# Experts' rows turned by a transposing transfer instead of TensorE and a copy

## The reference

```python
xn = _layernorm(x)
# attention: 16 heads of width 32, latent width 128, causal softmax, two output maps
attn = _L0_attn_ref(xn, Wq, Wdkv, Wuk, Wuv, ln_g, ln_b, Wo_h, Wo, bo)
# experts: 8 experts of 512 x 512, each token takes the mean of its best two
gate_logits = einsum('nsd,de->nse', xn, gate_w) + gate_b
_, top_idx = top_k(gate_logits, 2)
all_out = relu(einsum('nsd,edo->nseo', xn, expert_w) + expert_b)
sel = take_along_axis(all_out, top_idx[..., None], axis=2)
return x + attn + sel.mean(axis=2)
```

## Time and profile before

| | us |
|---|---|
| median of 3 runs | 1585.38 (1584.78 to 1585.88) |
| the profiled execution | 1584.98 |
| its span, first to last instruction | 1583.2 |
| experts' stage, first product to last | 1269.45 to 1494.38 |
| TensorE busy over the span | 1505.3 (95%) |
| VectorE | 1138.1 (72%) |
| ScalarE | 901.9 (57%) |
| GpSimd | 579.8 (37%) |

### The profile page before, as it was taken

How to read it: one execution, slowest core, us unless ns; L and a number is a source line. 1 busy time by engine, 2 the same in 40 slices (tenths; PEclk the granted TensorE clock), 3 DMA queues, 4 the chain that set the end, 5 groups by cost and what they waited for, 6 DMA issues and landing times.

```text
span 1583.2 us, 42974 instructions
## 1 busy us (share of the span) xinstructions
PE 1505.3 (95%) x12544; PEld 809.7 (51%) x12545; DVE 1138.1 (72%) x2385; ACT 901.9 (57%) x1629; POOL 579.8 (37%) x725
## 2 busy tenths in 40 slices
PE   5799989999999999999999999999999999999998
PEld 2788844444444444444444444444444445555443
DVE  4788768887777777777777877777777434444478
ACT  1677736666666666666666666666666733333200
POOL 2444402222454544433222322223222466666400
PEclk8799969999999999999999999999999999999999
DMA  6489861222332223222232223222332256655499
GB/s 157 163 267 269 236 172 56 70 71 62 87 83 71 65 68 93 72 70 65 79 90 67 69 68 95 72 68 64 85 85 72 53 172 216 203 163 171 148 410 358
DMA packets 156337, 198.06 MB, mean 125 GB/s; under 512 B 45280, under 2 KB 94560, under 8 KB 155904
## 3 DMA queue, kind: packets, MB, share of 16 engines
q1 hardware_dynamic: 114720, 98.23, 21.9%
q10 hardware_dynamic: 27936, 61.38, 12.5%
q0 software_dynamic: 13632, 37.87, 7.4%
HBM read 109.13 MB, written 63.12 MB: 109 GB/s over the span
## 4 chain that ended last, share of the span: by engine, by line
PE 78%; DVE 9%; DMA 4%; issue 4%; SPq 3%; ACT 1%; another core or an unknown queue 1%; POOL 1%; DVEq 0%; ACTq 0%; POOLq 0%
PE PS L1342 29%; PE PS L1397 28%; PE PS L1447 11%; PE PS L1471 5%; DVE pm L1131 5%; PE PS L1429 2%; DMA arena<-in_x 1%; SPq L428 1%; DVE mx L1136 1%; SPq L420 1%; DVE mx L1135 0%; DVE arena L993 0%; PE PS L1288 0%; PE PS L1259 0%
## 5 line engine op out<-in xcount | busy, mean ns | idle before, releaser
L1131 DVE TENSOR_REDUCE pm<-PS 128x1 f32<-128x512 f32 (+3 forms) x1280 | 716.5, 601 | 201.6 <-PE PS L1342 190.8
L866 ACT ACTIVATE arena<-PS 128x512 f32<-128x512 f32 (+1 forms) x1152 | 613.5, 574 | 302.1 <-PE PS L1342 278.7
L1342 PE MATMUL PS<-arena 97*64 97x512 f16 (+7 forms) x5120 | 695.2, 353 | 28.6 <-DVE pm L1131 21.0
L1397 PE MATMUL PS<-arena 128*33 128x512 f32 (+3 forms) x2560 | 634.9, 531 | 1.0 <-POOL arena L650 1.0
L1342 PEld LDWEIGHTS PS<-arena 97*64 97x64 f16 (+1 forms) x5120 | 330.4, 110 | 417.3 <-DVE pm L1131 138.4
L650 POOL TENSOR_SCALAR_AFFINE_SELECT arena<-arena 128x256 f32<-128x256 f32 (+1 forms) x256 | 111.1, 434 | 548.9 <-ACT arena L866 547.8
L1397 PEld LDWEIGHTS PS<-arena 128*33 128x33 f32 x2560 | 159.4, 111 | 80.6 <-POOL arena L650 1.7
L1447 PE MATMUL PS<-w_hi,arena 128*128 x576 | 171.5, 379 | 4.1 <-DVE arena L1198 1.8
L885 ACT ACTIVATE arena<-PS 128x1024 f16<-128x1024 f32 x72 | 73.4, 1024 | 148.6 <-remote 109.7
L1342 PE MATMUL PS<-later,deny 128*64 128x128 f16 x1024 | 146.1, 222 | 0.0
L1198 DVE SCALAR_TENSOR_TENSOR arena<-PS,eb_bc 128x512 f32<-128x512 f32 x72 | 49.8, 691 | 119.8 <-remote 61.3
(11 more groups left out here) (174 smaller groups left out, 1283.3 us busy)
## 6 DMA issues: line engine op xcount, KB each, us to landing
comb_hl<-arena SPq DMA_DIRECT2D x256, 64.0 KB
w_hi<-expert_rows ACTq DMA_DIRECT2D x32, 512.0 KB, 7.6
arena<-q_pieces ACTq DMA_DIRECT2D x90, 128.0 KB
arena<-k_pieces ACTq DMA_DIRECT2D x90, 128.0 KB
v_rows<-w_lo SPq DMA_DIRECT2D x8, 1056.0 KB, 7.3
arena<-in_x SPq DMA_DIRECT2D x16, 512.0 KB, 5.8
xn_rows<-arena SPq DMA_DIRECT2D x16, 512.0 KB, 6.2
q_pieces<-w_hi SPq DMA_DIRECT2D x32, 256.0 KB, 5.2
```

The source lines that it names most:

```text
L866: a.activation(probs[kk % 4][:, a_ * CH:a_ * CH + w], PS[:, s2_bank(k, x), 0:w], ACT.Exp, scale=SCALE).then_inc(s["exp_done"], 1)
L1131: v.reduce_max(pm[:, c, r, p:p + 1], PS[:, S1_BANK[n], 0:w], AX).then_inc(s["s1_done"], 1)
L1342: last = t.matmul(PS[h:h + P // 2, bank, cols], lhsT[:, h:h + P // 2], rhs, start=start, stop=stop)
L1397: last = t.matmul(PS[rows_, 6 + c % 2, CH - wds[a]:CH], v_sb[pu % 2][:, j + a, :], probs[pk % 4][:, a * off:a * off + wds[a]], start=p_ in ...
```

## The change

The tile's gathered rows are turned by one DMA transfer, from `x_g[n % 4]` to `xg_T[n % 4]`, issued by ScalarE. TensorE's `turn`, its two pairs of PSUM banks and ScalarE's copy are gone. `xg_T` grows from two buffers to four. ScalarE waits for the gather (`xg_in`) and for the product four tiles before (`z_ps`), then issues. GpSimd's gather waits for the transfer four tiles before (`gT0` to `gT3`, one semaphore for each buffer), TensorE's product for its own. Since two of the four buffers lie where attention has its data, ScalarE waits once, before tile 3, for the last moves of attention (`ot_out`). TensorE's loop takes all 18 passes.

```diff
@@ buffers @@
+        xg_T += [tD(2 * KB * P, f16).rearrange("p (z k c) -> p z k c", z=2, k=KB) for _ in range(AHEAD_G - len(xg_T))]
@@ GpSimd, gather @@
-                pool.wait_ge(s["gt_ps"], count(n - AHEAD_G + 1))
+                if n >= AHEAD_G:
+                    pool.wait_ge(s[f"gT{q}"], count(n // AHEAD_G * 16))
@@ ScalarE @@
-            def turned(n, u):
-                act.wait_ge(s["gt_ps"], count(n + 1))
-                act.wait_ge(s["z_ps"], count(n - 1))
-                a.activation(xg_T[u].rearrange("p z k c -> p (z k c)"),
-                             PS[:, 4 + 2 * u:6 + 2 * u, :].rearrange("p z c -> p (z c)"), ACT.Copy).then_inc(s["gT_done"], 1)
-
-            for n in range(2 * (BESIDE + 1)):
-                turned(n, n % 2)
+            def turned(i, q, ever):
+                act.wait_ge(s[f"xg_in{q}"], (i + 1) * 16)
+                if ever:
+                    act.sem_inc(s["step_at"], 1)
+                act.wait_ge(s["z_ps"], count((i - 1) * AHEAD_G + q + 1))
+                if ever:
+                    act.sem_inc(s["step_at"], 1)
+                act.dma_start_transpose(xg_T[q].rearrange("p z k c -> p (z k) c"), x_g[q]).then_inc(s[f"gT{q}"], 16)
+
+            for n in range(2 * AHEAD_G):
+                if n == AHEAD_G - 1:
+                    for par in range(2):
+                        act.wait_ge(s[f"ot_out{par}"], count(BH * OT_OUT))
+                turned(n // AHEAD_G, n % AHEAD_G, False)
             high_part(BH - 1)
-            with act.Fori(BESIDE + 1, PT // 2) as i:
-                for u in range(2):
-                    turned(i * 2 + u, u)
+            with act.Fori(2, PT // AHEAD_G) as i:
+                for q in range(AHEAD_G):
+                    turned(i, q, True)
@@ TensorE @@
-            def turn(n, i, q):
-
-                u = q % 2
-                pe.wait_ge(s[f"xg_in{q}"], (i + 1) * 16)
-                pe.wait_ge(s["gT_done"], count(n - 1))
-                for z in range(2):
-                    for k in range(KB):
-                        last = t.matmul(PS[:, 4 + 2 * u + z, k * P:(k + 1) * P], x_g[q][:, z * E + k * P:z * E + (k + 1) * P],
-                                        ident16[:], start=True, stop=True)
-                last.then_inc(s["gt_ps"], 1)
-
-            def experts(i, more):
+            def experts(i):
                 for q in range(AHEAD_G):
                     n, u = i * AHEAD_G + q, q % 2
-                    if q < AHEAD_G - 1 or more:
-                        turn(n + 1, i + (q + 1) // AHEAD_G, (q + 1) % AHEAD_G)
                     e = pe.value_load(expert_of[0:1, ds(n, 1)], min_val=0, max_val=NE - 1)
-                    pe.wait_ge(s["gT_done"], count(n + 1))
+                    pe.wait_ge(s[f"gT{q}"], count((i + 1) * 16))
                     pe.wait_ge(s["half_done"], count(n - 1))
...
-                        last = t.matmul(PS[:, u, :], xg_T[u][:, z, k, :],
+                        last = t.matmul(PS[:, u, :], xg_T[q][:, z, k, :],
...
-            turn(0, 0, 0)
             pe.wait_ge(s["ot_done"], count(NC * BH))
-            with pe.Fori(0, PT // AHEAD_G - 1) as i:
-                experts(i, True)
-            experts(PT // AHEAD_G - 1, False)
-
-
-            pe.wait_ge(s["gT_done"], count(PT))
+            with pe.Fori(0, PT // AHEAD_G) as i:
+                experts(i)
```

More of the change, by code:

```diff
@@ L218, in layer_kernel @@
             "cnt_ps routed id_zero id_done ids_in "
-            "xg_in0 xg_in1 xg_in2 xg_in3 gt_ps gT_done z_ps half_done y_done y_st0 y_st1 y_st2 y_st3 "
+            "xg_in0 xg_in1 xg_in2 xg_in3 gT0 gT1 gT2 gT3 z_ps half_done y_done y_st0 y_st1 y_st2 y_st3 "
             "proj_ps acc_done dveE"
```

## The result

The changed kernel takes 1613.45 us (median of 4 runs, 1603.88 to 1618.63) against 1585.63 us for the kernel before beside it: ratio 1.017, 95% interval 1.013 to 1.021. It is 1.7% slower, clear of the noise, and lies above the range of the prediction (1550 to 1602 around 1569). Its profiled execution has a span of 1612.0 us, 28.8 more than before's 1583.2.

What follows compares the result with a forecast made beforehand. TensorE bounds the experts' stage at 3.12 us a tile; without turning, GpSimd's steps (gain 15.9 us) and TensorE's stalled products (gain 14.5) both give about 2.91 a tile, so 1584.98 less 15.5 is 1569, range 1550 to 1602.

Steps and rivals of the forecast that it cites:

- I take 0.80: Experts' stage: a transposing transfer of 256 KB takes 0.80 us of all 16 DMA engines, as a gather does.
- The strided load: Load of ln_g in 4-byte elements, used as upper limit on the transfer's cost: 250 us a tile.
- the sentence from the Trainium skill on equal speed: Transposing transfers run as fast as ordinary ones, 350 to 400 GB/s; the transfer's term would be 0.7 us.
- Landing "3.15": Start of the experts' stage: tile 0's transfer lands 3.15 us after its issue, like a 256 KB load.
- 0.9 us later: Start of the experts' stage: first product at 1270.4 instead of 1269.45, 0.9 us later.
- The stall of 0.64 us in every second tile: TensorE's two product banks: a VectorE signal 2.3 us late stalls TensorE 0.64 us in every second tile.
- 72 x 2.91: TensorE's forecast path through the experts' stage: 72 tiles at 2.91 us, ending at 1479.9 against 1494.38.
- GpSimd's 1.46 us a step: Gathers and scatters in the experts' stage: 133 steps of 1.46 us, 2.92 us a tile.
- the rival of TensorE's bound: Experts' stage: GpSimd's steps stay at 1.28 us and signals come in time; 33 us less, 1552; chance 24%.
- The round trip (14%): Gather plus transfer above 11.6 us makes the ring of four set the pace; at 14 us, 1612; chance 14%.
- The slow blocks' 4 us a tile: Transposing transfer works block by block, not by bytes; at 4 us a tile 1650; chance 12%.
- ScalarE's issues: ScalarE gains 72 transfer issues, taken at 1.23 us each, well below a tile's 2.9.

Runs made afterwards that it cites:

- r4_after: Changed kernel with four product banks in place of two: 1.0234 of the kernel before, 1607.9 us.
- r4_copy: Changed kernel with a plain copy in place of the transposing transfer and four product banks in place of two: 0.9891 of the kernel before, 1557.7 us.
- e11_copy_store: Changed kernel with a plain copy for the transposing transfer and SyncE's plain stores for GpSimd's scatters, two product banks: 0.9803 of the kernel before.
- e2_half_block: Changed kernel with only the high pieces of the rows turned and used, 128 KB a tile: 1.0120 of the kernel before.
- e1_plain_copy: Changed kernel with a plain copy of the same 256 KB in place of the transposing transfer: 1.0114 of the kernel before.
- e4: Kernel before with an extra plain copy of 256 KB a tile for 68 tiles, issued by SyncE into spare buffers: 1.0044 of the kernel before.
- e9: Kernel before with every second tile turned by the transposing transfer, the others by TensorE, and four product banks: 1.0049 of the kernel before.
- e12: Changed kernel with a plain copy for the transposing transfer and TensorE's, ScalarE's and VectorE's loops written out, two product banks: 1.0087 of the kernel before.
- e15: Transposing transfer for every fourth of the first 32 tiles, every second of the last 40; turning two products ahead, four banks: 1.0083 of the kernel before.
- e14_fourth_two_ahead: Kernel before with every fourth tile by the transposing transfer, TensorE's turning written two products ahead, four product banks: 0.9963 of the kernel before.

## Why the prediction was wrong

- **"I take 0.80"** for the transposing transfer's work. It was 1.72 us, and the estimate had only a lower end that was near: the plain copy's 0.71 us is what the forecast was made for. The DMA share was 1.03 where 83% was forecast, and without any late signal the transposing kind cost 50 us against the plain one (`r4_after` against `r4_copy`). This is the step that failed first: on a chip without late signals it alone turns the gain (0.989) into a loss (1.023). On the chips with late signals it isn't the whole, since a plain copy was slower than before there too (1.011 and 1.009). The strided load bounded it from above so far out that I went by likeness instead; the sentence from the Trainium skill on equal speed ("Advanced Engine Details and Errata", X-Bar Transpose) is not borne out by these runs: 1.3 to 2.1 us against 0.71.
- **Landing "3.15"**, first product "0.9 us later". It was 6.35 us from issue to product, and 3.9 us later.
- **The stall of 0.64 us in every second tile**: 72 x 2.91 less 186.6 is 22.9 us in all, and TensorE's waits for VectorE measured 23.3 (30.8 with the plain copy). The sum was near, by luck: the lateness doesn't come about every second tile (over 1 us at 20 of 72 products before, at 18 after), and a late signal costs more than 0.64 us. That it came as 10 to 14 waits of up to 4 us was not foreseen, and so neither was the next point. On two of the chips the lateness is absent.
- **The clock was counted at nothing.** The products ran on from gaps at the lower level: 22.3 us, and 15.1 with the plain copy. This term was missing altogether, and with four banks and a plain copy (clock 0.99) it was 4.
- From the forecast stage of 72 x 2.91 = 209.5 us to the 249.74 measured, 40.2: 22.3 of clock, 16.5 of waits for transfers, and 1.4 of small differences. The waits for VectorE that were forecast (22.9) and measured (23.3) cancel. With 3.0 for the later start (1273.36 for 1270.4) that is 43 of the 45 us between 1569 and the profiled execution (1613.8).
- **GpSimd's 1.46 us a step** was too slow: with four banks and the plain copy 72 tiles took 195.49 us, 2.72 a tile or 1.36 a step, while TensorE was busy for 190.56 us of them, so GpSimd didn't bind. With a plain copy and no late signals the rival of TensorE's bound comes near: a stage of 195.5 us against the 191 of the rival. `e11_copy_store`, at 0.9803 of before, is 1554 here, and the rival had 1552.
- **The round trip (14%)** had the time, 1612, and a pace of 3.5 us (249.74 / 72 = 3.47), but only half of the way to it: the transfers' share of the idle time was 16.5 us. The rest is late signals and clock, so its number was partly luck. The slow blocks' 4 us a tile weren't reached; but that the kind of transfer and not its bytes sets its cost, their mechanism, is what `r4_after` against `r4_copy` shows.
- Right were: the removal of the turning, the unchanged last stage, ScalarE's issues (1.28 us each in the median, 1.23 taken), and, on the chip of the result, that lateness of signals is what TensorE meets once the turning no longer lies between two products. What the turning had covered was seen there, but not what a ring of two banks without it costs beside the stall itself.

## What to carry to other kernels

Measure the engine time of one transfer of a new kind before 72 of them depend on it, beside the traffic that it will meet; one plain copy in its place tells its work from everything else. Taking work off the bounding engine also takes away the time that this work gave to its signals: where the trace shows a consumer starting 2 us late, count on waits there. Price a gap on TensorE at more than its length when the matmuls behind it show the lower clock. And before a cure is credited, look in its trace whether the ill was there at all: a ratio to the kernel before on the same chip doesn't help when the chip decides how late the signals are and the two kernels don't suffer from it alike.

## What the runs showed of the hardware

- A transposing transfer of 256 KB took 1.72 us of the 16 DMA engines in some 1,054 packets of about 249 bytes in the changed kernel, 1.3 to 2.1 us in the others; a plain copy of the same size 0.70 to 0.71 us, in 144 packets. Half the block (128 KB) took 19.3% for 29 transfers, 0.67 us (`e2_half_block`).
- On the chips of the result, of `e1` to `e4`, of `e9` to `e12` and of `e15` TensorE's signals reached VectorE up to 5.8 us late (18 of 72 over 1 us in the changed kernel), in `e1_plain_copy` 1.2 to 1.7 us after the end of one of GpSimd's issues where it was over 3 us. With half as many indirect DMAs none was late on such a chip (`e11_copy_store`). On the two other chips no signal was late, in rows of up to 67 issues.
- In the changed kernel's stage pairs of matmuls took 1.03 to 1.06 us behind gaps of 3.12 to 6.69 us, and 0.60 behind those up to 2.35 us. In `e1_plain_copy` two gaps of 2.77 us were followed by either: 0.60 at 1400.77, 1.03 at 1414.07.
- Gathers and scatters took 0.91 us of the DMA engines beside the transposing transfers in the changed kernel, from 0.79 (`e14_fourth_two_ahead`) to 1.00 (`e2_half_block`) in the others; 0.80 before and 0.77 in `r4_copy`, without them.
